# A wait for four scatters' landing ahead of the four gathers of each turn, in a graph network's edge loop

## The chip, the cores and the metric

The kernel runs on one core of a Trainium2 chip. Its time is the device time of one execution in microseconds (us), and the figure for a kernel is the median of its timed runs.

## What is computed

One message-passing step on a graph of 50,000 nodes with 128 features and 50,000 edges with 16 attributes, all float32; `src` is sorted by `dst`:

```python
edge_input = concat([x[row], x[col], edge_attr])          # row = src, col = dst
m_ij = silu(silu(edge_input @ eW1 + eb1) @ eW2 + eb2)
agg = segment_sum(m_ij, row, num_segments=50000)
update = silu(concat([x, agg]) @ nW1 + nb1) @ nW2 + nb2
out = layernorm(x + (x + update))
```

## The kernel before

The work has three stages.

**Plan.** DVE works out for each edge the bucket of its source node (80 nodes a bucket), and PE and DVE check that the fast form fits this graph. ACT meanwhile fills the HBM array `table` with empty slots. POOL issues the first gathers, and builds constants.

**Edge loop.** The edges, padded to 98 groups of 512 (four tiles of 128), are worked off in 98 turns, g = 0 to 97. A turn has these parts on the engines:

- SP loads `place`, `attr` and four windows of `x` for the destination nodes (lines 264, 268, 276).
- PE turns the gathered source rows (`turn_src`, L476, one group ahead, `s_src_turned`), picks the destination rows (`turn_dst`, L488), computes the edge network (L514, L518, L520, L525), ranks the edges within their buckets (`rank_mm`, L502 and L505) and makes q, the message times the second half of nW1 (L530, `s_q_mm`).
- ACT makes hT and mT (L590, L593) and copies xdT (L584).
- DVE makes the one-hot rows, finds the ranks (L761) and the slots (`find_pos`, L769, `s_pos`), and copies q from PSUM to one of Q = 10 buffers (`copy_q`, L774 and L776, `s_q`). Its copy of group g waits until the scatters of group g - 10 have landed (`s_scattered`).
- POOL runs `scatter(g)` (four indirect DMAs of 128 rows of 132 values to `table`, L381) and `gather_src(g + LEAD)` with LEAD = 22 (four indirect DMAs of 128 rows of `x` to one of X_SRC = 18 buffers, L340). `scatter(g)` waits for `s_q` and `s_pos`. `gather_src(h)` waits until PE has turned group h - 18, which for h = g + 22 is group g + 4. For h of 98 and over it does nothing, so the last 22 turns, g = 76 to 97, have no gathers.

The semaphore of a scatter's landing, `s_scattered[g % 10]`, rises by 16 for each of the four DMAs of a group. It is waited for by DVE in `copy_q` and by SP ahead of the node stage (L323).

**Node stage.** For 79 blocks of 640 nodes SP loads `x`, `xT` and the slots of `table` (L311, L313, L317), PE sums the slots by node and runs the node network (L546, L549, L559), POOL adds a bias (L435) and raises variances to a power (L441), DVE takes moments, ACT scales and stores.

The queues of all engines are in program order; the order is that of the code.

Of the kernel before, what the change touches and what calls it, by code (L numbers as in the profile page):

```python
# [7 lines left out]
TILES = 4  # L8
# [25 lines left out]
Q = 10  # L34
# [13 lines left out]
def gnn_kernel(nc, x, xT, src_col, src_idx, dst_idx, dst_g, attrT, w1s, w1d, w1a, eb1, w2, eb2, nw1a, nb1, nw1b, nw2, nb2,  # L48
# [22 lines left out]
    with ExitStack() as ctx:  # L71
# [3 lines left out]
        def sem(name):  # L75
            return ctx.enter_context(nc.semaphore(name))
# [96 lines left out]
        s_scattered = [sem(f"s_scattered{s}") for s in range(Q)]  # L173
# [18 lines left out]
        def wait(eng, s, value):  # L192

            if value > 0:
                eng.wait_ge(s, value)
# [137 lines left out]
        def _(pool):  # L333
# [5 lines left out]
            def gather(rows, idx, g, t, done):  # L339
                pool.indirect_dma_start(  # L340
                    rows, None, x[:, :], bass.IndirectOffsetOnAxis(ap=idx[:, g * TILES + t:g * TILES + t + 1], axis=0)
                ).then_inc(done, 16)

            def gather_src(g):

                if g >= GROUPS:
                    return
                wait(pool, s_src_turned, g - X_SRC + 1)
                for t in range(TILES):
                    gather(x_src[g % X_SRC][:, t * D:(t + 1) * D], idx_src, g, t, s_gathered[g % X_SRC])  # L350
# [25 lines left out]
            def scatter(g):  # L376

                wait(pool, s_q, 2 * (g + 1))
                wait(pool, s_pos, g + 1)
                for t in range(TILES):  # L380
                    pool.indirect_dma_start(  # L381
                        table[:, :], bass.IndirectOffsetOnAxis(ap=pos[:, g * TILES + t:g * TILES + t + 1], axis=0),
                        q[g % Q][:, t, :], None,
                    ).then_inc(s_scattered[g % Q], 16)
# [18 lines left out]
            with pool.If_eq(pool.to_reg(fit), 1):  # L403
                for g in range(X_SRC, LEAD):
                    gather_src(g)
                pool.wait_ge(s_fill, 16 * len(FILL_BLOCKS))
                for g in range(GROUPS):
                    scatter(g)
                    gather_src(g + LEAD)
            with pool.Else():  # L410
                for s in range(WINDOWS):
# [464 lines left out]
```

## Time and profile before

| | us |
|---|---|
| median of three timed runs | 1614.44 (1608.35 to 1617.39) |
| profiled execution | 1598.11 |
| its span, first to last instruction | 1596.6 |
| mean granted TensorE clock in it | 0.923 |
| first and last scatter's start | 153.3, 1259.1 |
| last gather's start | 1066.4 |

Times within the profiled execution count from the start of its span. A gap "[idle before <- who]" is the engine's idle time ahead of an instruction and who ended it; "remote" is an update whose maker the profile doesn't tell. "Issue" is time in which an engine waited for nothing that the profile shows. Starts of PE's products are recorded and their ends are modelled.

### The profile page before, as it was taken

The numbers are of one execution on the slowest core, as the hardware profiler recorded it, in microseconds if no ns is written. First come the engines' busy times: TensorE is split into PE (matmuls) and PEld (weight loads), VectorE is DVE, ScalarE is ACT, GpSimd is POOL, SyncE is SP. The second block draws the span as 40 slices with busy tenths as digits, with TensorE's granted clock in tenths as the row PEclk, the third lists the DMA queues.
The fourth block names the chain that finished last, engine by engine and source line by source line (L and its number), as shares of the span: only waits on it lengthen the run. The fifth ranks groups of instructions, "written<-read, shape, count | busy, mean of one in ns | idle before, by whom it ended". The sixth has DMA issues, their size and how long they took to land.

```text
span 1596.6 us, 24603 instructions
## 1 busy us (share of the span) xinstructions
PE 1304.5 (82%) x7491; PEld 886.1 (56%) x7491; DVE 937.9 (59%) x2976; ACT 443.4 (28%) x766; POOL 1043.0 (65%) x956
## 2 busy tenths in 40 slices
PE   1109888888888888888888888878999699999996
PEld 1005554454454454545455455545666499998995
DVE  9104554554554554554554555546677388888886
ACT  0001111111111111111111111111222177777776
POOL 8763666666666666666666666663443488887885
PEclk9558999999999999999999999998999899999998
DMA  9995333333333333333333333332333499999995
GB/s 379 410 413 172 99 100 106 102 99 101 107 98 102 109 98 106 101 101 105 99 105 101 102 103 102 101 107 81 106 111 94 156 358 383 383 381 365 382 384 227
DMA packets 156842, 284.94 MB, mean 178 GB/s; under 512 B 28046, under 2 KB 92322, under 8 KB 156708
## 3 DMA queue, kind: packets, MB, share of 16 engines
q1 hardware_dynamic: 110020, 162.78, 31.3%
q10 hardware_dynamic: 21600, 68.32, 10.6%
q0 software_dynamic: 25088, 52.23, 10.2%
q8 instruction: 62, 1.02, 0.3%
q14 instruction: 72, 0.59, 0.1%
HBM read 188.31 MB, written 94.91 MB: 177 GB/s over the span
## 4 chain that ended last, share of the span: by engine, by line
PE 31%; DVE 28%; another core or an unknown queue 28%; issue 8%; SPq 4%; DMA 1%; POOL 0%; ACT 0%; ACTq 0%; POOLq 0%
DVE junk L761 14%; PE psum L549 9%; PE psum L559 6%; DVE onehot L753 6%; PE psum L546 5%; DVE pick L743 4%; DVE xsT L734 2%; PE psum L488 2%; PE psum L502 1%; PE psum L505 1%; PE psum L525 1%; SPq L275 1%; PE psum L514 1%; PE psum L530 1%
## 5 line engine op out<-in xcount | busy, mean ns | idle before, releaser
L340 POOL DMA_INDIRECT x_src<-x_d,idx_src x392 | 391.5, 999 | 269.3 <-PE psum L476 149.2
L381 POOL DMA_INDIRECT table<-q,pos x392 | 395.9, 1010 | 199.7 <-issue 113.7
L761 DVE CUSTOM_DVE_ANT_0 junk<-onehot,psum 128x625 f16<-128x625 f16 x392 | 299.1, 800 | 74.2 <-PE psum L505 62.2
L776 DVE COPY q<-psum 128x512 f32<-128x512 f32 x98 | 67.8, 692 | 459.8 <-remote 425.7
L502 PE MATMUL psum<-onehot,after 128*128 128x512 f16 (+1 forms) x780 | 183.9, 320 | 155.1 <-DVE rank L761 153.6
L488 PEld LDWEIGHTS psum<-pick,window 128*128 128x128 f32 x1568 | 201.4, 200 | 95.3 <-issue 95.3
L488 PE MATMUL psum<-pick,window 128*128 128x128 f32 x1568 | 198.7, 282 | 33.7 <-issue 33.7
L502 PEld LDWEIGHTS psum<-onehot,after 128*128 128x128 f16 x780 | 55.2, 100 | 283.0 <-issue 268.8
L505 PE MATMUL psum<-onehot,before 128*128 128x512 f16 (+1 forms) x784 | 187.1, 324 | 0.0
L441 POOL TENSOR_TENSOR rstd<-var_eps,minus_half 128x5 f32<-128x5 f32 (+1 forms) x79 | 134.5, 1703 | 74.0 <-DVE var_eps L821 74.0
L590 ACT ACTIVATE hT<-psum,b_e 128x512 f32<-128x512 f32 x98 | 67.3, 687 | 401.5 <-remote 184.1
L549 PEld LDWEIGHTS psum<-owner,slots_in 128*128 128x128 f32 x1250 | 153.0, 193 | 12.6 <-issue 0.4
L608 ACT ACTIVATE y_out<-y,shift,rstd 128x128 f32<-128x128 f32 x391 | 155.9, 476 | 1.5 <-ACT y_out L608 0.9
L593 ACT ACTIVATE mT<-psum,b_e 128x512 f32<-128x512 f32 x98 | 67.3, 687 | 315.8 <-PE psum L525 230.1
L549 PE MATMUL psum<-owner,slots_in 128*128 128x80 f32 x1250 | 150.1, 273 | 0.0
L514 PE MATMUL psum<-attr,w_attr 16*128 16x512 f32 x196 | 110.9, 645 | 37.6 <-issue 36.4
L753 DVE TENSOR_SCALAR onehot<-bucket_ids,bucket 128x625 f16<-128x625 f16 x392 | 136.5, 412 | 0.0
L525 PE MATMUL psum<-hT,w_e 128*128 128x512 f32 x196 | 132.1, 762 | 2.1 <-ACT hT L590 2.1
L600 ACT ACTIVATE uT<-psum,b_n 128x640 f32<-128x640 f32 (+1 forms) x79 | 108.0, 1367 | 87.8 <-PE psum L549 87.3
L584 ACT COPY xdT<-psum 128x512 f32<-128x512 f32 x98 | 57.4, 585 | 238.2 <-remote 166.3
L435 POOL TENSOR_TENSOR base<-x_in,half_n 128x640 f32<-128x640 f32 (+1 forms) x79 | 120.3, 1525 | 0.0
L546 PE MATMUL psum<-xT_in,w_self 128*128 128x320 f32 x314 | 98.7, 437 | 13.9 <-DVE owner L801 11.7
(92 smaller groups left out, 1520.9 us busy)
## 6 DMA issues: line engine op xcount, KB each, us to landing
window<-x_d SPq DMA_DIRECT2D x392, 128.0 KB
slots_in<-table SPq DMA_DIRECT2D x79, 528.0 KB, 6.2
table<-empty ACTq DMA_DIRECT2D x9, 4224.0 KB
x_in<-x_d SPq DMA_DIRECT2D x78, 320.0 KB, 5.1
xT_in<-xT_d SPq DMA_DIRECT2D x78, 320.0 KB, 5.2
out<-y_out ACTq DMA_DIRECT2D x78, 320.0 KB, 5.4
place<-place_dram SPq DMA_DIRECT2D x98, 128.0 KB
x_src<-x_d,idx_src POOLq DMA_INDIRECT x392
```

What stands on the lines that cost most here:

```text
L340: pool.indirect_dma_start(rows, None, x[:, :], bass.IndirectOffsetOnAxis(ap=idx[:, g * TILES + t:g * TILES + t + 1], axis=0)).then_inc(don ...
L381: pool.indirect_dma_start(table[:, :], bass.IndirectOffsetOnAxis(ap=pos[:, g * TILES + t:g * TILES + t + 1], axis=0), q[g % Q][:, t, :], None,
L441: pool.tensor_tensor(rstd[b % Y][0:p, 0:r], var_eps[b % Y][0:p, 0:r], minus_half[0:p, 0:r], ALU.pow).then_inc(s_rstd, 1)
L488: last = nc.tensor.matmul(p_dst[:, t * P:(t + 1) * P], window[g % WINDOWS][:, t, r * D:(r + 1) * D], pick[g % 2][:, r, t * P:(t + 1) * P], ...
L502: nc.tensor.matmul(count[:, cols], after[:], earlier[:, cols], start=False, stop=False, skip_group_check=True)
L505: last = nc.tensor.matmul(count[:, cols], before[:], onehot[g % 2][:, t, cols], start=n < 2, stop=True, skip_group_check=True)
L525: nc.tensor.matmul(p_hm, w_e2[:], hT[g % 2][:], start=True, stop=True).then_inc(s_m_mm, 1)
L546: nc.tensor.matmul(u[a], w_self[:], xT_in[b % X_IN][:, a * n:(a + 1) * n], start=True, stop=True)
L549: last = nc.tensor.matmul(u[k * BUCKET // n][:, o:o + BUCKET], slots_in[b % SLOTS_IN][:, k, 0:D], owner[b % 3][:, k, :], start=False, stop ...
L608: last = nc.scalar.activation(y_out[b % 3][0:p, j * D:(j + 1) * D], y[b % Y][0:p, j * D:(j + 1) * D], ACT.Identity, bias=shift[b % Y][0:p, ...
L753: last = V.tensor_scalar(onehot[g % 2][:, t, :], bucket_ids[:], bucket[:, c:c + 1], None, ALU.is_equal)
L761: V.tensor_tensor_reduce(out=junk[t % 2][:], in0=onehot[g % 2][:, t, :], in1=p_rank[t % 2], scale=-step if t % 2 else step, scalar=0.0, op ...
```

## The change

After the four scatters of a turn POOL waits until all four have landed, and goes on to the wait and the gathers of `gather_src` only then. The count, 16 x 4 x (g // 10 + 1), is the one that group g brings its semaphore to. The wait stands in all 98 turns, those without gathers too.

```diff
                 for g in range(GROUPS):
                     scatter(g)
+                    pool.wait_ge(s_scattered[g % Q], 16 * TILES * (g // Q + 1))
                     gather_src(g + LEAD)
```

## Rows read from the trace of the kernel before

**Rows 1.** The page: busy us (share of the span) and instructions by engine.
```profile
PE 1304.5 (82%) x7491; PEld 886.1 (56%) x7491; DVE 937.9 (59%) x2976; ACT 443.4 (28%) x766; POOL 1043.0 (65%) x956
```

**Rows 2.** Four stretches: length, each engine's busy time, granted clock, DMA share, GB/s.
```profile
330.00:500.00 170.00, 143.94 (x734) 86.01 (x734) 92.09 (x256) 27.65 (x43) 112.11 (x113) 0.93 0.34 102
1062.00:1092.00 30.00, 18.11 (x91) 10.93 (x88) 13.61 (x37) 3.75 (x6) 15.83 (x16) 0.77 0.27 78
1092.00:1250.00 158.00, 158.00 (x897) 99.70 (x897) 113.32 (x309) 33.33 (x51) 68.14 (x71) 1.00 0.37 108
1280.00:1590.00 310.00, 300.11 (x2263) 275.96 (x2261) 253.96 (x1081) 244.11 (x466) 246.36 (x154) 0.99 0.98 365
```

**Rows 3.** DVE's copies of q (line L776), with gathers and without.
```profile
L776 DVE COPY q<-psum x76: 691/692/693, 155.3 to 1061.6; 128x512 f32<-128x512 f32 x76
...
L776 DVE COPY q<-psum x19: 691/692/692, 1091.4 to 1254.3; 128x512 f32<-128x512 f32 x19
```

**Rows 4.** POOL's timeline: start, duration, line, operation, idle time before it.
```profile
171.78 0.98 POOL L340 DMA_INDIRECT x_src<-x_d,idx_src  x1 [1.68 <-PE psum L476]
...
700.70 0.98 POOL L340 DMA_INDIRECT x_src<-x_d,idx_src  x1 [2.16 <-PE psum L476]
...
705.87 1.20 POOL L381 DMA_INDIRECT table<-q,pos  x1 [0.30 <-issue]
...
709.93 0.96 POOL L381 DMA_INDIRECT table<-q,pos  x1 [0.30 <-issue]
712.62 0.98 POOL L340 DMA_INDIRECT x_src<-x_d,idx_src  x1 [1.72 <-remote]
...
721.77 0.96 POOL L381 DMA_INDIRECT table<-q,pos  x1 [0.30 <-issue]
724.97 0.98 POOL L340 DMA_INDIRECT x_src<-x_d,idx_src  x1 [2.23 <-PE psum L476]
```

**Rows 5.** What ended POOL's idle time before gathers (L340), 155 to 1066 us.
```profile
  PE psum L476: 124.9, 62
...
  remote: 24.9, 14
```

**Rows 6.** The timeline of all engines in one turn.
```profile
705.32 1.06 PE L530 MATMUL psum<-w_agg,mT 128*128 128x128 f32 x8
...
712.12 0.69 DVE L776 COPY q<-psum 128x512 f32<-128x512 f32 x1 [5.77 <-remote]
```

**Rows 7.** The chain that ended last, 1240 to 1265 us: start, length, what.
```profile
1246.29 0.70 DVE q L776
1246.99 0.27 issue
...
1259.08 2.29 DMA table<-q,pos
...
1261.38 0.03 SPq L323
```

**Rows 8.** DMA issues: size and median time from issue to landing.
```profile
slots_in<-table SPq DMA_DIRECT2D x79, 528.0 KB, 6.2
```

**Rows 9.** POOL's timeline where the gathers stop.
```profile
1067.67 1.20 POOL L381 DMA_INDIRECT table<-q,pos  x1 [0.31 <-issue]
...
1081.94 0.97 POOL L381 DMA_INDIRECT table<-q,pos  x1 [0.31 <-issue]
1092.33 0.97 POOL L381 DMA_INDIRECT table<-q,pos  x1 [9.43 <-DVE q L776]
```

**Rows 10.** The timeline of all engines there: DVE's and ACT's rows.
```profile
1073.88 0.69 DVE L776 COPY q<-psum 128x512 f32<-128x512 f32 x1 [5.73 <-remote]
...
1085.22 0.69 ACT L590 ACTIVATE hT<-psum,b_e 128x512 f32<-128x512 f32 x1 [16.44 <-remote]
...
1091.36 0.69 DVE L776 COPY q<-psum 128x512 f32<-128x512 f32 x1 [3.00 <-PE psum L530]
```

**Rows 11.** POOL's waits after 1062 us: total, times, longest.
```profile
POOL table L381 <- DVE q L776: 86.0, 19, 9.4
```

## The prediction

> **What bounds the kernel now.** I read the page first. PE is busy 82% of the span and POOL 65% [rows 1], averages over three unlike stages that say nothing of where an added wait on POOL would tell. The edit runs once in each of the 98 turns of the edge loop, so the edge loop is the stage to read, and its first 76 turns (g = 0 to 75) apart from its last 22, since gathers are issued only while g + 22 < 98.
>
> The table of stretches and the copy of q by DVE (one a turn) give the two paces. With gathers there are 76 copies between 155.3 and 1061.6 us: 906.3 / 75 = 12.08 us a turn, at a granted clock of 0.93 to 0.94 and with PE busy about 84%. Without gathers 19 copies between 1091.4 and 1254.3: 162.9 / 18 = 9.05 us a turn, clock 1.00, PE busy 100% [rows 2, 3]. So PE is the bound only in the last turns. In the first 76 something adds 3 us to each.
>
> POOL's timeline says what. A turn of POOL is four gathers and four scatters back to back, and then a pause: from 712.62 to 721.77 + 0.96 = 722.73 us it issues (10.11 us), it rests 2.23 us, and goes on at 724.97. The turns before and after begin 11.9 and 12.4 us apart, as the loop does [rows 4]. The 76 pauses together are 124.9 + 24.9 = 149.8 us, 1.97 us each, and 62 of them are ended by PE's transpose L476, the event that gather_src waits for (gather g + 22 needs the transpose of g + 4) [rows 5]. Why PE is late with it shows in the whole timeline at the same place: PE's product L530 started at 705.32 and should let DVE copy q at 706.4, but the copy starts at 712.12, 5.77 us idle before it, which is 1.23 us after POOL's last scatter ended (709.93 + 0.96 = 710.89) [rows 6]. DVE, ACT and POOL all go on within half a microsecond there. What PE reports late is seen about when a run of eight indirect DMAs has drained. I can't name the mechanism from these rows; what matters is the circle: PE's news comes 1.2 to 1.7 us after POOL's run ends, POOL restarts on that news, and 10.11 + 1.97 = 12.08 us is the turn. In these 76 turns a delay of POOL's restart would therefore pass into the end at its full size. Elsewhere POOL has room.
>
> **The change, part by part.** Nothing is removed or moved. One wait is added to each of 98 turns, between the fourth scatter and the wait of gather_src. Queued behind it on POOL: four gathers (then the next four scatters). Who waits for those: PE's transpose of group g + 22, some 17 turns later, and DVE's copy_q ten groups later, both with tens of microseconds to spare; and, through the circle above, everybody. SP's and ACT's queues are not touched.
>
> *How late is a landing?* The edge loop's trace shows no landing of a scatter. The last one of the program does: issued at 1259.08, landed 2.29 us later, and SP's wait for it ends at 1261.38. POOL was done with the instruction after 0.96 us, so the landing is 1.33 us behind POOL's own end [rows 7]. *What does a restart take?* DVE's copy ends at 1246.99 and POOL's scatter starts 0.27 us later [rows 7]. So the new wait alone would let POOL go on 1.33 + 0.27 = 1.60 us after its last scatter. The shortest pauses now are 1.68 to 1.72 us, others 2.2, the mean 1.97 [rows 4, 5]. The landing falls inside the pause, with 0.1 us to spare in the tightest turns and 0.4 in the mean.
>
> Bounds of this step: below, 0 (a satisfied wait is free: POOL passes two of them, for q and pos, between its last gather and first scatter at 705.87, and the gap is the same 0.30 us as between any two of its DMAs [rows 4]). It can't be a gain here, as the restart still needs the old news too. Above, a landing as slow as that of the slots' load, 6.2 us from issue [rows 8]: 6.2 - 0.96 + 0.27 - 1.97 = 3.5 us a turn, 269 us. I take the near end: that load moves 528 KB in a stretch where the DMA engines are busy 0.98, while in the edge loop they are busy 0.34 to 0.35 with gathers and 0.37 without, where 1.33 was read [rows 2]. For the tight turns, where the landing may come a little behind the news now and then, I put 0.02 us on each of 76: **+1.5 us**.
>
> The Trainium skill, "DMA: Bandwidth & Descriptors", section "Anatomy of one DMA — SWDGE (gpsimd) path", gives 2.0 us plus the bytes over 436 GB/s; for 67,584 bytes that is an estimate of 2.16 us, near the row's 2.29, and by it this step would be 0 as well. The same page warns in that section that the completion "can cause a surprisingly long delay especially when the write target is HBM", and in "Latency and other measured facts" puts HBM's latency at 0.2 us on average and 2 us at high load; the table is such a target. If it were 1.8 us more here, an estimate of 76 x (1.33 + 1.8 + 0.27 - 1.97) = 109 us would be lost. That is the first rival; no row of this loop speaks for that load.
>
> *Turns 76 to 78.* Gathers have stopped, POOL is three groups behind and issues twelve scatters without rest, 1067.67 to 1081.94 + 0.97 = 1082.91, behind the four gathers before [rows 9]. In this run DVE's copies of q stand at 1073.88 and 1091.36: one turn of 17.48 us, with ACT idle 16.44 us until 1085.22, again some 2 us after POOL stopped, and the clock of the stretch down at 0.77 [rows 2, 10]. The new wait puts a rest of about 1.6 us behind each group, as long as the pauses in which PE's news comes through now. The groups would then be issued from 1067.67, 1074.3, 1080.7 and 1087.1, each 4.8 us long, and POOL has caught up with DVE by group 80. If runs of four don't hold PE up (they don't in the last turns, 9.05 us each), this turn is 17.48 - 9.05 = 8.4 us shorter; if it is like a turn with gathers, 17.48 - 12.08 = 5.4 us; if POOL's run has nothing to do with it, 0. It can't lose, as nothing waits for these three groups' scatters until DVE takes up their buffers ten groups later. I take a little over the middle of the first two less a chance of the third: **-6 us**.
>
> *Turns 79 to 97.* POOL waits 86.0 us for DVE over these 19 groups, 9.4 us at the first and (86.0 - 9.4) / 18 = 4.3 us at each of the others [rows 11]; a landing of 1.33 us lies inside. **0.** At the end POOL sees the last landing at about 1261.4 instead of starting on the node stage at 1260.06; its first sum is wanted only after the first slots have come through PE (the load is issued at 1261.57), so **0** again.
>
> **The sum**, against the profiled execution of 1598.11 us (span 1596.6): +1.5 - 6 = -4.5, so 1593.6 us, or -0.28%. That execution is 1% below the median of the three timed runs, 1614.44; the same 4.5 us off that median is **1610 us**.
>
> **The rivals.**
> *First, the landing is later than PE's news (slower).* Place: each of 76 pauses. It decides as soon as the mean landing is over 1.97 - 0.27 = 1.70 us behind POOL's last scatter instead of 1.33, and in the tight turns from 1.42. For it: POOL's scatter queue stands behind four gathers and beside SP's window loads in the loop, which the last landing of the program did not. Against it: the equal DMA share. At a landing of 2.0 us: 76 x 0.3 = 23 us, less 6: 1631 us. Chance 0.15.
> *Second, the wait changes nothing at all.* The landing is always there before the news, and the 17.48 us turn is no matter of POOL's rest: 1614 us, perhaps 1616 with the tight turns. For it: I have one such turn in one execution. Chance 0.25.
> *Third, PE's news is held by scatters in flight, and a wait on them frees the loop.* Were the first 76 turns to fall toward 9.05 us, up to 76 x 3.0 = 230 us would be gained; at a tenth of it, 1587 us. Against it: POOL rests at this very place already, and the scatters have landed by then. Chance 0.05.
> *My forecast*, the loop unchanged and the catch-up shorter: 1610 us, by itself 1604 to 1615. Chance 0.55.
>
> **Range and chances.** The forecast and the second case are within 1604 to 1617, allowing for the spread of the timed runs, 1608.35 to 1617.39. The first rival's small end reaches 1624. From 1601 to 1624 leaves some 2 in 10 out, most of it above. A measurement of this kernel tells about 0.5%, or 8 us, from no change. Faster by more than that: the third rival, the forecast at its full 8.4 us and spread, 0.16. Slower by more: the first rival and spread, 0.16. Within it: 0.68.
>
> **What would show it.** In the changed kernel's trace: the 76 pauses before the gathers still near 1.97 us in the mean, now partly put down to the scatter's landing; 12.1 us between copies of q; no POOL run of over eight DMAs, gaps of about 1.6 us behind groups 76 to 78, and no 17 us turn there; the last 19 turns at 9.05; node stage the same length. I am wrong if the pauses are over 2.1 us in the mean, if the pace with gathers leaves 12.0 to 12.2, or if the long turn stays with the rests in place.

## The result, and the profile after

The changed kernel takes 1641.9 us in the median of four runs (1640.89 to 1644.42), the kernel before 1612.58 in four: ratio 1.0183, interval 1.015 to 1.0216. I had forecast 1610 us in a range of 1601 to 1624: the forecast was wrong in size and sign, and the range missed. The profiled execution after took 1642.03 us, 43.9 more than that of before; the medians differ by 29.3, since the execution profiled before was 1% quicker than its median.

POOL's gathers and scatters over the whole kernel, and the page's head, after: operation, count, duration in ns (least, median, most), first and last start in us.

```profile
span 1640.3 us, 24679 instructions
...
L340 POOL DMA_INDIRECT x_src<-x_d,idx_src x392: 940/947/14050, 3.8 to 1117.5; - x196
...
L381 POOL DMA_INDIRECT table<-q,pos x392: 963/970/1218, 155.0 to 1302.3; - x196
```

With the starts of the profile before (last gather 1066.4 and last scatter 1259.1 from its table, first gather behind a scatter at 160.0 from the same trace), the 43.7 us of span fall so: up to the first gather behind a scatter +2.3 (162.3 against 160.0); the 76 turns with gathers (1117.5 - 162.3) - (1066.4 - 160.0) = **+48.8**; from there to the last scatter 184.8 - 192.7 = **-7.9**; node stage 338.0 - 337.5 = +0.5. The loss is in the turns with gathers, but for 2.3 us ahead of them, and the last turns do give something back.

DVE's copies of q and what ended POOL's idle time ahead of the gathers, after (they answer to [rows 3] and [rows 5]; the added line moves the numbers of the lines below it up by one, L476 to L477, L776 to L777, and later edits move them further):

```profile
L777 DVE COPY q<-psum x76: 691/692/693, 158.4 to 1111.7; 128x512 f32<-128x512 f32 x76
...
  remote: 95.9, 38
  PE psum L477: 94.8, 35
...
  DMA table<-q,pos: 7.8, 3
```

A turn takes (1111.7 - 158.4) / 75 = 12.71 us against 12.08, and the 76 pauses 198.5 us, 2.61 each against 1.97. So POOL's pause grew by 0.64 us, where I had allowed 0.02. The profile puts three of the pauses down to the scatter's landing, the others to PE's transpose (L477 here) or to an update without a maker. That count alone settles little, as this trace holds only 1,649 of the 6,272 updates by landed scatters. The step from PE's update to the gather does: it is 0.80 to 0.81 us in all 76 turns, the three included. Had a landing come last anywhere, the step would be longer there. So what was added is not waiting for the landing. PE's and POOL's timelines show it, first before, then after:

```profile
724.10 0.60 PE L476 MATMUL psum<-ident,x_src 128*128 128x128 f32 x4
```

```profile
706.06 0.60 PE L477 MATMUL psum<-ident,x_src 128*128 128x128 f32 x4
707.48 0.99 POOL L340 DMA_INDIRECT x_src<-x_d,idx_src  x1 [3.44 <-PE psum L477]
```

Before, the transpose ends at 724.70 and the gather starts at 724.97 [rows 4], 0.27 us later. After, it ends at 706.66 and the gather starts at 707.48, 0.82 us later. In the traces' records of semaphore updates the step from PE's update to the gather is 0.26 us in all 76 turns of before, and 0.80 to 0.81 in all of after. The reader can see where the half microsecond comes from in the instructions that waited on POOL at this place in the changed kernel, at 716 to 721 us, ahead of a gather at 719.99:

```profile
L195 POOLq EVENT_SEMAPHORE  x1: 17/17/17, 719.2 to 719.2; - x1
```

In all of these traces a gather carries one wait itself. The first gather of a turn had one, for `s_src_turned`, and carried it. Now it has two. It carries the one that stands first in the program, the new wait for the landing, and the wait for PE's transpose has become an instruction of its own ahead of it (line 195, the helper of that wait). That one passes at 719.2, within 0.05 us of PE's update, and the DMA behind it starts 0.76 us after its end. The Trainium skill, "Perfetto Trace Analysis", section "Identifying Dependency Chains", says that an instruction that waits on several engines may get EventSemaphore instructions with the additional waits ahead of it. The trace agrees, with the one at 719.2.

### The profile page after: what moved, and what is told of

It is laid out like the page before. It is cut to its first block, busy times and chain, and to the rows that moved or that the text cites. A ratio compares the mean times of both kernels' runs of the same rounds, so it can differ in the third digit from the quotient of the medians.

```text
span 1640.3 us, 24679 instructions
## 1 busy us (share of the span) xinstructions
PE 1314.8 (80%) x7491; PEld 892.8 (54%) x7491; DVE 944.5 (58%) x2976; ACT 443.4 (27%) x766; POOL 1042.9 (64%) x956
## 4 chain that ended last, share of the span: by engine, by line
PE 32%; another core or an unknown queue 28%; DVE 28%; issue 7%; SPq 3%; DMA 1%; ACT 0%; POOL 0%; ACTq 0%; POOLq 0%
DVE junk L762 13%; PE psum L550 8%; PE psum L560 5%; PE psum L547 5%; DVE onehot L754 5%; DVE pick L744 4%; PE psum L489 3%; DVE xsT L735 2%; PE psum L503 2%; PE psum L506 2%; PE psum L515 1%; PE psum L526 1%; PE psum L531 1%; PE psum L519 1%
## 5 line engine op out<-in xcount | busy, mean ns | idle before, releaser
L340 POOL DMA_INDIRECT x_src<-x_d,idx_src x392 | 391.8, 999 | 320.2 <-PE psum L477 121.2
L777 DVE COPY q<-psum 128x512 f32<-128x512 f32 x98 | 67.8, 692 | 501.7 <-remote 468.8
L489 PEld LDWEIGHTS psum<-pick,window 128*128 128x128 f32 x1568 | 208.6, 206 | 104.2 <-issue 62.6
L489 PE MATMUL psum<-pick,window 128*128 128x128 f32 x1568 | 204.5, 287 | 41.3 <-DMA window<-x_d 41.3
L550 PEld LDWEIGHTS psum<-owner,slots_in 128*128 128x128 f32 x1250 | 154.1, 194 | 12.8 <-issue 0.8
L609 ACT ACTIVATE y_out<-y,shift,rstd 128x128 f32<-128x128 f32 x391 | 155.9, 475 | 1.5 <-ACT y_out L609 0.9
L754 DVE TENSOR_SCALAR onehot<-bucket_ids,bucket 128x625 f16<-128x625 f16 x392 | 132.4, 403 | 0.0
L744 DVE TENSOR_SCALAR pick<-place,row_f 128x512 f32<-128x512 bf16 x196 | 96.2, 531 | 41.0 <-issue 23.3
```

Source lines behind the costliest of these rows:

```text
L340: pool.indirect_dma_start(rows, None, x[:, :], bass.IndirectOffsetOnAxis(ap=idx[:, g * TILES + t:g * TILES + t + 1], axis=0)).then_inc(don ...
L489: last = nc.tensor.matmul(p_dst[:, t * P:(t + 1) * P], window[g % WINDOWS][:, t, r * D:(r + 1) * D], pick[g % 2][:, r, t * P:(t + 1) * P], ...
L550: last = nc.tensor.matmul(u[k * BUCKET // n][:, o:o + BUCKET], slots_in[b % SLOTS_IN][:, k, 0:D], owner[b % 3][:, k, :], start=False, stop ...
L609: last = nc.scalar.activation(y_out[b % 3][0:p, j * D:(j + 1) * D], y[b % Y][0:p, j * D:(j + 1) * D], ACT.Identity, bias=shift[b % Y][0:p, ...
L744: last = V.tensor_scalar(pick[g % 2][:, r, :], place[g % 2][:], row_f[:, r:r + 1], None, ALU.is_equal)
L754: last = V.tensor_scalar(onehot[g % 2][:, t, :], bucket_ids[:], bucket[:, c:c + 1], None, ALU.is_equal)
```

## The experiments

The kernel before took 1595 to 1613 us in some sets of runs and 1379 to 1380 us in others, and every ratio below is against the kernel before in its own set. The two are told apart in the last section of this part; I call them the held loop (1600 us) and the free loop (1380 us). The recorded comparison is of the held loop. The first three sets were of the free loop, which nothing in my trace had let me expect.

"PE's news" is PE's update behind the transpose, for which the gather waits. Theory A: the order of the two waits costs, since the news, which comes last, is no longer waited for by the gather itself. Theory B: the landing comes late. Theory C: the rest behind each scatter group does away with the turn of 17.5 us. Theory D, formed after the first set: in the free loop POOL never rests, so there every wait lies bare.

**A wait that is always fulfilled, first in order.**

```diff
                     scatter(g)
+                    pool.wait_ge(s_idx_src, 16)
                     gather_src(g + LEAD)
```

> The landing wait is replaced by a wait for the load of the source indices, fulfilled since the start of the kernel; it stands at the same place, in all 98 turns, so the first gather of a turn again carries two waits, and PE's transpose is the one that comes last. Theory A (two waits on one indirect DMA: in the changed kernel the gather starts 0.80 us after PE's news instead of 0.26, because that news is waited for in a wait instruction of its own ahead of the DMA, and the landing has no part in it): pauses of 2.5 to 2.6 us, 12.7 us a turn, the long turn of 17.5 us stays; 1598 + 48 = 1646 us profiled, ratio to before 1.030. Theory B (the landing comes late): pauses of 1.97 us as before, ratio 1.000.

Measured in the free loop: 1380.64 against 1379.24 us, ratio 1.0011 (1.0002 to 1.0019). Run again, twice.

> The wait fulfilled long before, ahead of the wait for PE's transpose, in all turns. Where the kernel before takes some 1610 us: theory A says 0.54 us a turn with PE's transpose in a wait instruction of its own (restart 0.80 us behind the news instead of 0.26), 41 us, ratio 1.025; the landing has no part. If the landing had been what cost in the changed kernel, 1.000. Where it takes 1380 us: 1.001 as the first time.

The second was of the free loop too: 0.9998 (0.9984 to 1.0012).

> As satisfied_first_2: 1.025 by theory A where the kernel before takes some 1610 us, 1.000 if the landing was what cost there; 1.000 where it takes 1380 us.

The third met the held loop: 1622.47 against 1594.8 us, **ratio 1.0176** (1.0153 to 1.0198), with no wait for a landing anywhere. The changed kernel's ratio is 1.0183. What ended the pauses ahead of the gathers:

```profile
  remote: 94.3, 42
  PE psum L477: 76.5, 34
```

They add up to 170.8 us, 2.25 each, and the step from PE's update to the gather is 0.80 us in the mean, where the kernel before has 0.26. Theory B alone falls: it said 1.000. Theory A said 1.025 and got the sign and some two thirds of the size: the pause grew by 0.28 and not by 0.54, because PE's news came 0.27 us earlier behind POOL's last scatter (1.44 against 1.71 us in the mean). I don't know why it did.

**The same wait, last in order**, so that the gather carries PE's transpose again:

```diff
                 wait(pool, s_src_turned, g - X_SRC + 1)
+                pool.wait_ge(s_idx_src, 16)
```

> The fulfilled wait for the source indices stands behind the wait for PE's transpose, so that it gets the wait instruction of its own, passed at once when POOL comes to it, and the gather carries PE's transpose. Theory A: pauses of 1.97 us, ratio 1.000. A rival, A2 (any second wait on an indirect DMA costs 0.5 us, in whatever order): pauses of 2.5 us, ratio 1.030. Theory B: 1.000.

> The same fulfilled wait behind the wait for PE's transpose. Where the kernel before takes some 1610 us: 1.000 by theory A, as the gather carries PE's transpose again; 1.025 if any second wait costs. Where it takes 1380 us: 1.001.

Both in the free loop: 1.0008 (0.9998 to 1.0017) and 1.0011 (0.9994 to 1.0028). A second wait that is fulfilled costs nothing there in either order. In the held loop this kernel wasn't met.

**The landing wait behind the wait for PE's transpose**, in the 76 turns with gathers alone:

```diff
-            def gather_src(g):
+            def gather_src(g, scattered=None):
...
                 wait(pool, s_src_turned, g - X_SRC + 1)
+                if scattered is not None:
+                    pool.wait_ge(s_scattered[scattered % Q], 16 * TILES * (scattered // Q + 1))
...
-                    gather_src(g + LEAD)
+                    gather_src(g + LEAD, scattered=g)
```

> POOL waits for the landing in the 76 turns with gathers alone, and behind the wait for PE's transpose, not ahead of it. By the order of the waits in the program the landing gets the wait instruction of its own and PE's transpose is carried by the gather. Theory A: the gather is ready some 0.77 us after the landing's wait ends, 1.4 + 0.8 = 2.2 us, or 0.26 us after PE's news, whichever is later: pauses of 2.2 to 2.3 us, 12.3 us a turn, 1598 + 20 = 1618 us profiled, ratio 1.012. Theory B (the landing comes late): the order of two waits is of no matter, pauses of 2.6 us as in the changed kernel, ratio 1.030 with the catch-up's gain away.

Free loop: 1531.62 against 1379.24 us, 1.1102 (1.1084 to 1.112), outside both expectations, and the run that sent me to look for theory D.

> The kernel swap once more, on whatever chip this is. Where the kernel before takes 1380 us: 1.110 as the first time, pauses of 2.5 us. Where it takes 1612 us and the pauses are 1.97 us: by theory A 1.012.

Held loop: 1624.18 against 1607.34 us, **1.0097** (1.0067 to 1.0128), pauses of 2.34 us in the mean (177.9 us). This kernel waits for the same two things as the changed one in these turns and loses 17 us instead of what would be some 37 (29.3 and the 8 given back in the last turns). The gather starts 0.26 us behind PE's news or 0.80 us behind the landing, whichever is later; in some 60 of the 76 turns it is the second. Here every landing can be read, since its wait is an instruction of its own: it passes 1.33 to 1.83 us behind the last scatter's end, 1.44 in the mean. So the prediction's 1.33 was near in this loop too.

**The kernel before once more**, for a trace of the free loop:

> The kernel before, unchanged, for a trace of it from the chip of these experiments, on which it takes 1379 us and not 1612. In the three kernels of the first round that don't wait in the loop POOL never rests there, and PE's news comes on time. Theory D (the pause of 1.97 us that I read as the wait's cover exists only where PE's news comes late; here there is none): pauses of 0.30 us, the copies of q 9.1 us apart until POOL is ten groups behind, then 10.4, ratio 1.000. Rival: this chip is faster all over, with pauses of 1.97 us scaled down.

1379.79 us, ratio 1.0001 (0.9991 to 1.001). DVE's copies of q in two stretches, and two stretches of the engines (columns as in [rows 2]):

```profile
L776 DVE COPY q<-psum x62: 683/692/692, 136.8 to 696.3; 128x512 f32<-128x512 f32 x62
...
L776 DVE COPY q<-psum x19: 679/684/685, 737.9 to 926.0; 128x512 f32<-128x512 f32 x19
```

```profile
300.00:600.00 300.00, 300.00 (x1712) 190.19 (x1711) 221.15 (x593) 64.69 (x99) 229.53 (x232) 1.00 0.44 128
730.00:920.00 190.00, 171.61 (x948) 104.30 (x946) 118.79 (x329) 35.85 (x55) 145.78 (x146) 1.00 0.40 118
```

```profile
POOL x_src L340 <- issue: 116.7, 383, 0.3
POOL table L381 <- issue: 116.2, 381, 0.3
...
POOL x_src L340 <- PE psum L476: 9.8, 9, 4.2
POOL table L381 <- DVE q L776: 2.7, 9, 0.3
```

The third fence is POOL's waits. It hardly waits for anything: 12.5 us for PE and DVE in the whole loop, and 0.3 us of issue between any two of its DMAs. PE is busy all of the time at full clock, a copy of q comes every 9.17 us, (696.3 - 136.8) / 61, and POOL, at some 10.4 us a turn, falls behind until DVE has no free buffer of the ten. From about 700 us the pace is POOL's: (926.0 - 737.9) / 18 = 10.45 us. There is no pause here in which a landing could hide.

**The changed kernel, the landing wait with gathers only, without gathers only, and both with the other order:**

```diff
# loop_only
+                    if g + LEAD < GROUPS:
+                        pool.wait_ge(s_scattered[g % Q], 16 * TILES * (g // Q + 1))
# tail_only
+                    if g + LEAD >= GROUPS:
+                        pool.wait_ge(s_scattered[g % Q], 16 * TILES * (g // Q + 1))
# swap_all: swap, and the two lines of tail_only
```

> The changed kernel, unchanged. Theory D: here the landing of 1.3 to 2.9 us and the restart lie bare in each of the 76 turns with gathers, and POOL is the bound. Turn of POOL: 9.9 + the landing, 1.75 in the mean, + a restart of 0.3 to 0.8 us behind it = 12.2 us against 10.4; and another 2 us behind each of the last 22 groups. 76 x 2.2 + 22 x 1.6 = 200 us at most, less what DVE's ten buffers hide at the start; from the ratios of swap, 1.110, and tail_only, 1.026: 1.13 to 1.14, 1560 to 1570 us. Theory A (only the order of the waits costs, 0.5 us a turn): 1.030. If the chip is again one with 12.08 us a turn, 1.018.

> The landing wait ahead of the gathers alone, in the order of the changed kernel: PE's transpose has the wait instruction of its own and the landing is carried by the gather. Theory D: as swap, 1.110, if anything 1.10, since the gather starts 0.3 us behind a landing that it carries itself and 0.8 us behind one that has its own instruction: pauses of 2.1 us in the mean against 2.5, 76 x 0.4 = 30 us less, 1500 us. Theory D2 (the order is of no matter to the restart): 1532 us as swap.

> The landing wait only in the 76 turns with gathers, in the changed kernel's order. Where the kernel before takes some 1610 us: 48 us as in the changed kernel without the catch-up's 8 us gain, ratio 1.028 to 1.030. Where it takes 1380 us: 1.089.

> As swap, and the landing wait in the 22 turns without gathers too. With the gathers' part as in swap (1532 us) and the last turns' part as in tail_only (36 us) the two add up to 1568 us, ratio 1.137. If POOL's lag is already made good before the loop ends, the last turns cost less than in tail_only.

> POOL waits for the landing only in the 22 turns without gathers. Theory C (the rest behind each group of four breaks the run of sixteen indirect DMAs that holds PE's news up): the turn of 17.5 us is gone as in the changed kernel, 8 us less, 1590 us profiled, ratio 0.995. Rival (that turn has another cause, and its absence in the changed kernel comes of the slower loop): the long turn stays, ratio 1.000.

> The landing wait only in the 22 turns without gathers. Where the kernel before takes some 1610 us (POOL waits 86 us for DVE there): no wait is exposed, the turn of 17.5 us falls to 9 to 12 us, 8 us less, ratio 0.995. Where it takes 1380 us (POOL lags ten groups behind there): 1.026.

All in the free loop:

| kernel | us | before | ratio (interval) | mean pause, 76 turns |
|---|---|---|---|---|
| changed kernel | 1536.13 | 1380.21 | 1.1142 (1.1109 to 1.1174) | 2.09 us |
| loop_only | 1502.73 | 1380.21 | 1.0886 (1.0866 to 1.0906) | 2.10 us |
| loop_only again | 1506.0 | 1379.37 | 1.0917 (1.0897 to 1.0937) | 2.18 us |
| swap (above) | 1531.62 | 1379.24 | 1.1102 (1.1084 to 1.112) | 2.52 us |
| swap_all | 1567.85 | 1380.21 | 1.1364 (1.1338 to 1.1389) | 2.48 us |
| tail_only | 1415.09 | 1379.24 | 1.0263 (1.025 to 1.0276) | 0.31 us |
| tail_only again | 1414.79 | 1379.37 | 1.0252 (1.0233 to 1.0271) | 0.30 us |

The two places add up: 122.5 (loop_only) + 35.8 (tail_only) = 158.3, measured 155.9; 152.4 (swap) + 35.8 = 188.2, measured 187.6. And the order of the two waits alone is 152.4 - 122.5 = 30 us, as theory D had it, or 0.39 us in each of 76 turns (26 us by the second run of loop_only). Here it's the other order that is dear, since here the landing is what comes last. POOL's waits in loop_only, and one pause in the chain that ended last of swap:

```profile
POOL x_src L340 <- DMA table<-q,pos: 157.8, 75, 4.3
```

```profile
1012.03 2.42 DMA table<-q,pos
1014.44 0.02 issue
1014.47 0.02 POOLq L350
1014.49 0.76 issue
1015.25 0.98 POOL x_src L340
```

In swap the landing is waited for by an instruction of its own (line 350), and the gather starts 0.76 us behind it. In loop_only the gather carries that wait, and by the record of updates it starts 0.26 us behind the last of the 64 in all 76 turns. My 1560 to 1570 us for the changed kernel was too much because I had priced its order as swap's.

> As tail_only_2: where the kernel before takes some 1600 us, 8 us less, ratio 0.995, and no turn of over 13 us behind the last gathers; where it takes 1380 us, 1.026.

Held loop: 1588.43 against 1596.26 us, **ratio 0.9953** (0.9936 to 0.997), as forecast. The turn of 17.5 us is gone: the longest step between two copies of q behind turn 74 is 13.3 us, a little over the 13 that I had allowed, and in the profile of the changed kernel it is 12.8. The kernels of the held loop that have no wait in the last turns all keep a long one: 17.9 us in swap_again, 20.8 in satisfied_first_3, 16.8 in after_gathers. The rests stand behind each group (POOL's timeline, first scatter of groups 76 to 79):

```profile
1068.35 1.21 POOL L381 DMA_INDIRECT table<-q,pos  x1 [0.30 <-issue]
...
1075.17 0.96 POOL L381 DMA_INDIRECT table<-q,pos  x1 [1.79 <-DMA table<-q,pos]
...
1081.54 0.97 POOL L381 DMA_INDIRECT table<-q,pos  x1 [1.58 <-DMA table<-q,pos]
...
1088.75 0.96 POOL L381 DMA_INDIRECT table<-q,pos  x1 [2.42 <-DMA table<-q,pos]
```

**An old landing:** the wait stands where the changed kernel has it, but is for group g - 1.

```diff
+                    if g > 0:
+                        pool.wait_ge(s_scattered[(g - 1) % Q], 16 * TILES * ((g - 1) // Q + 1))
```

> POOL waits ahead of its gathers for the landing of the group before (g - 1), 10 us old by then: the added wait with its wait instruction, without the idle time. Theory D on a chip where POOL never rests (1380 us): ratio 1.000, pauses of 0.30 us. On one with 12.08 us a turn, by theory A: PE's transpose is again in a wait instruction of its own, 0.5 us a turn, ratio 1.03. Rival (a wait on a scatter's semaphore costs by itself): over 1.02 on either.

Free loop: 1380.12 against 1379.27 us, 1.0008 (0.9998 to 1.0019). It isn't the instruction that costs there, it is POOL's idle time.

**The landing wait in every second of the 76 turns:**

```diff
+                    if g + LEAD < GROUPS and g % 2 == 0:
+                        pool.wait_ge(s_scattered[g % Q], 16 * TILES * (g // Q + 1))
```

> The landing wait in every second of the 76 turns with gathers, none in the last 22. Theory D: POOL is the bound from its first scatter to its last, so that each rest counts at its full size and nothing is hidden by DVE's ten buffers: half of loop_only's 122 us, 1380 + 61 = 1441 us, ratio 1.044. Rival (the ten buffers take up a first part, some 75 us of lag, and only the rest shows): 38 x 1.8 = 68 us fit into it, ratio 1.00 to 1.01. With POOL's pauses exposed only where PE's news is early (12.08 us a turn), ratio 1.015.

Free loop: 1445.1 against 1379.27 us, 1.0494 (1.0459 to 1.0528), 65.8 us or 1.73 us a wait, against loop_only's 122.5 / 76 = 1.61 (1.67 in its second run). That is 5 us more than the half that I expected. It goes about in proportion, with no first part for free: the ten buffers of q hide none of it, since POOL works without a rest from its first scatter on and its lag only grows.

**The same wait one step later,** behind the gathers:

```diff
                     gather_src(g + LEAD)
+                    if g + LEAD < GROUPS:
+                        pool.wait_ge(s_scattered[g % Q], 16 * TILES * (g // Q + 1))
```

> The landing wait stands behind the four gathers of its turn, ahead of the next group's scatters, in the 76 turns with gathers. The landing comes 1.3 to 2.9 us behind the scatters and the gathers take 4.8 us, so it is always there. Theory D (what costs is POOL's idle time while it waits, not the wait): ratio 1.000, pauses 0.30 us. Rival (a third wait on the first scatter, which gets a second wait instruction ahead of it, lengthens the gap there): up to 0.5 us a turn, ratio 1.027.

Held loop: 1609.39 against 1607.34 us, 1.0011 (0.9985 to 1.0036). In the turns with gathers POOL still issues no scatter before the last group has landed, and pays nothing that can be measured for it: the four gathers cover the landing, and the gap ahead of the first scatter is 0.30 us as before. In the free loop this kernel wasn't met.

**What tells the two loops apart.** In the held loop PE's update behind L530, for which DVE's copy of q waits, is recorded 3.6 to 5.9 us after L530's end in the 60 turns of before between 170 and 900 us, 4.75 in the mean, when POOL's run of DMAs is over; in the last turns of that trace it is 0.01 us. In the free loop it is 0.01 us in all turns, although POOL runs without a rest. Two L530 of the free loop, an early one and one from where DVE waits for buffers:

```profile
409.10 1.06 PE L530 MATMUL psum<-w_agg,mT 128*128 128x128 f32 x8
410.19 0.69 DVE L776 COPY q<-psum 128x512 f32<-128x512 f32 x1 [1.44 <-PE psum L530]
...
701.86 1.06 PE L530 MATMUL psum<-w_agg,mT 128*128 128x128 f32 x8
...
706.54 0.17 DVE L774 COPY q<-local 128x4 f32<-128x4 f32 x1 [3.68 <-DMA table<-q,pos]
706.62 0.68 DVE L776 COPY q<-psum 128x512 f32<-128x512 f32 x1
```

The first copy starts 0.03 us behind L530's end. Before the second, DVE is held by the landing of a scatter ten groups back, and the copy that needs L530 follows at once; in [rows 6] it stood 5.7 us behind L530's end with nothing else to wait for. One thing in the traces goes with the two: the held loop's traces hold 15,000 to 16,000 semaphore updates (15,571 for the kernel before) and the free loop's 30,500 to 30,900 (30,616), of programs that make the same number; of the updates by landed scatters 1,963 of 6,272 are in the first and 6,192 in the second. It isn't the chip alone: one and the same chip gave the free loop in one set and the held loop in another. What makes the one or the other stays open.

## Why the prediction was wrong, point by point

**What bounds the loop.** The circle holds for the held loop: POOL's restart passes into the end at its full size (0.64 us more a pause, 0.63 us more a turn). What I added without a test, that a run of eight indirect DMAs holds PE's news up, is not a rule of the chip: in the free loop POOL's run has no end at all, and PE is not held. I had one trace of one condition.

**The step that failed** is "below, 0 (a satisfied wait is free ...)", and with it the +1.5 us for 76 turns. That term measured +48.8 us in the profiled pair. The landing was in time, as I had said: it decided none of the 76 restarts. The restart was not 0.27 us. I read that number from a DMA that carried the wait that came last, and the two fulfilled waits between gather and scatter from a place where nothing came last. I priced the landing and the old news each by itself and never asked which of the two the gather would carry. satisfied_first_3 shows that the order alone costs 27.7 us without a landing in play (25.2 in the turns with gathers of its profile, where the changed kernel has 48.8), and swap_again that the same two waits in the other order cost 17. What is left, 48.8 - 25.2 = 24 us by the profiled executions and 29.3 + 7.8 - 27.7 = 9 us by the medians, is not shown to be the landing wait's. It goes with when PE's news itself comes, behind POOL's last scatter: 1.81 us in the changed kernel and 1.44 in satisfied_first_3, where before has 1.71, and after_gathers, which costs nothing in the median, has 1.88 in its profiled execution. What moves it within the circle stays open.

**The catch-up, -6 us.** Right: -7.9 in the profiled pair, and tail_only_3 gives -7.8 us by itself, near the full 8.4.

**Turns 79 to 97 and the end, 0.** Right in the held loop, but for half a microsecond: the last group's first scatter starts 0.76 us behind DVE's copy (1297.76 to 1298.52 in the profile after), not 0.27, as it now carries the landing wait of the group before and the wait for the copy has an instruction of its own. In the free loop these turns cost 36 us, as POOL is behind and never waits for DVE there.

**The rivals.** None was the cause. The first, the landing later than the news, had 0.15, its price (23 us less 6, 1631 us) came near the measured time, and its mechanism was wrong: the landing was not later than the news, the restart behind the news was slower. That it came near is luck. In the free loop it is right and dear: there is hardly ever news to wait for, the landing comes 1.8 us behind the scatters in the mean, and the changed kernel loses 11%. Of the second, the long turn's part is refuted by tail_only_3; that the landing never ends a pause in the changed kernel was right, and didn't make the wait free. The third, the wait frees the loop, is refuted by the changed kernel's 12.71 us a turn.

**What I had said would show me wrong** did: the pauses are over 2.1 us and the pace left 12.0 to 12.2.

**A kernel that beats both?** tail_only does in the held loop (0.9953) and loses 2.5% in the free loop, so I wouldn't take it. Nothing beat the kernel before in the free loop.

## What to carry to other kernels

Adding a wait can cost more than the thing waited for: look which wait the instruction carries, and let it be the one that ends last; the others get instructions of their own, and the DMA starts half a microsecond further behind those. Put a wait behind work that the same engine has anyway, as after_gathers does. And a pause that covers an edit is worth a question of its own, whether it is there in every run; here the same edit cost 2% where there was a pause and 11% where there was none.

## What the runs showed of the hardware

- POOL's indirect DMA starts 0.26 us behind the last update when it carries that wait itself, and 0.80 us behind it (0.76 behind the wait instruction's end) when a separate wait instruction stands ahead: before, after, loop_only and swap, in all 76 turns of each, in both loops.
- A landing of four scatters of 128 rows comes 1.3 us behind POOL's last instruction when the loop is over, 1.4 us in the mean in the held loop (swap_again), and 1.7 to 1.8 us in the mean, up to 4.0, in the free loop (swap, loop_only).
- The kernel before runs at 1380 us or at 1595 to 1613 us, 16 to 17% apart, with its clock at 0.966 or 0.92 in the mean; in the slower case PE's update for the copy of q comes some 5 us late in the turns with gathers, in which POOL issues eight indirect DMAs in a row, and on time in the last turns. That fewer updates are recorded then goes with it; which of the two makes the other, or what makes both, no run here shows.
